# Row maxima of two heads on the two row halves of TensorE, with the attention loop written out

## The reference

```python
q = (x @ Wq.T)  -> (2, 16 heads, 1024, 8);  k, v likewise
attn = softmax((q @ k.T) * 128 ** -0.5, axis=-1)     # 1024 x 1024 for each of 32 heads
attn = attn + rel_bias_table[idx]                    # bias added after the softmax
out  = attn @ v  -> layer norm, * gamma + beta
```

## Time and profile before

| | us |
|---|---|
| median of three runs | 735.07 (731.84 to 736.51) |
| the profiled execution | 732.73 |
| its span | 731.0 |
| PE busy / DVE busy / ACT busy / POOL busy | 676.8 / 533.7 / 381.1 / 104.7 |
| a round of the attention loop | 50.70 |
| the round in which the loop starts its second pass | 56.40 |

### The profile page before, as it was taken

How to read it: one execution, slowest core, us unless ns; L and a number is a source line. 1 busy time by engine, 2 the same in 40 slices (tenths; PEclk the granted TensorE clock), 3 DMA queues, 4 the chain that set the end, 5 groups by cost and what they waited for, 6 DMA issues and landing times.

```text
span 731.0 us, 11045 instructions
## 1 busy us (share of the span) xinstructions
PE 676.8 (93%) x3458; PEld 279.1 (38%) x3458; DVE 533.7 (73%) x956; ACT 381.1 (52%) x687; POOL 104.7 (14%) x100
## 2 busy tenths in 40 slices
PE   7998899999987999999999899999999999988997
PEld 5453545444663522332332232322323322324443
DVE  5579878638799868868868668778688688308744
ACT  3734223324102257767767467667677577882231
POOL 5920211001046220020020020010200202002000
PEclk9999999999999999999999899999999999999999
DMA  8000000000313112012030120030120000000000
GB/s 258 3 0 0 2 0 1 1 0 6 120 66 114 59 48 76 6 55 67 19 98 12 32 96 1 25 100 1 38 87 3 1 0 2 2 1 0 1 29 29
DMA packets 21416, 26.64 MB, mean 36 GB/s; under 512 B 3312, under 2 KB 12016, under 8 KB 21360
## 3 DMA queue, kind: packets, MB, share of 16 engines
q1 hardware_dynamic: 20496, 25.39, 10.8%
q0 software_dynamic: 144, 0.52, 0.2%
q10 hardware_dynamic: 720, 0.00, 0.1%
HBM read 21.52 MB, written 4.19 MB: 35 GB/s over the span
## 4 chain that ended last, share of the span: by engine, by line
PE 70%; DVE 21%; ACT 3%; issue 2%; DVEq 1%; POOL 1%; DMA 1%; POOLq 0%; ACTq 0%
PE banks L1434 17%; PE banks L1357 15%; PE banks L1420 14%; DVE negmax L1034 7%; PE banks L1160 6%; PE banks L1238 4%; PE banks L1281 3%; PE banks L1371 3%; PE banks L1229 2%; DVE arena L892 2%; PE banks L1173 2%; ACT arena L737 1%; DVE arena L942 1%; DVE arena L894 1%; PE banks L1475 1%
## 5 line engine op out<-in xcount | busy, mean ns | idle before, releaser
L1034 DVE TENSOR_REDUCE negmax<-banks 128x1 f32<-128x1024 f32 x256 | 300.5, 1218 | 67.0 <-PE banks L1357 65.8
L737 ACT ACTIVATE arena<-banks 128x512 f32<-128x512 f32 x512 | 271.7, 601 | 143.9 <-PE banks L1420 140.3
L1357 PE MATMUL banks<-arena 72*128 72x512 bf16 x512 | 154.8, 384 | 15.7 <-DVE negmax L1034 15.2
L1420 PE MATMUL banks<-arena 75*128 75x512 bf16 x512 | 159.3, 382 | 6.3 <-ACT arena L737 3.1
L1434 PE MATMUL banks<-arena 128*32 128x512 f32 x1024 | 137.2, 608 | 0.7 <-ACT arena L737 0.7
L1357 PEld LDWEIGHTS banks<-arena 72*128 72x128 bf16 x512 | 36.4, 97 | 146.8 <-DVE negmax L1034 68.1
L1420 PEld LDWEIGHTS banks<-arena 75*128 75x128 bf16 x512 | 48.3, 98 | 93.6 <-ACT arena L737 47.6
L501 POOL TENSOR_TENSOR rstd<-veps,neghalf 128x4 f32<-128x4 f32 (+1 forms) x24 | 27.1, 1129 | 241.4 <-DVE veps L808 189.6
L1238 PE MATMUL banks<-arena,bT 128*128 128x512 f32 x128 | 60.1, 593 | 1.6 <-ACT arena L591 1.6
L591 ACT ACTIVATE arena<-banks 128x512 f32<-128x512 f32 (+1 forms) x56 | 32.1, 595 | 49.3 <-PE banks L1160 19.3
L892 DVE TENSOR_SCALAR arena<-banks,bi 128x512 f32<-128x512 f32 x32 | 23.9, 746 | 33.0 <-PE banks L1238 33.0
(11 more groups left out here) (132 smaller groups left out, 638.2 us busy)
## 6 DMA issues: line engine op xcount, KB each, us to landing
arena<-qk_scratch SPq DMA_DIRECT2D x192, 48.0 KB
arena<-in_tab SPq DMA_DIRECT2D x8, 1024.0 KB, 6.9
qk_scratch<-arena SPq DMA_DIRECT2D x8, 384.0 KB, 2.7
out<-x SPq DMA_DIRECT2D x4, 256.0 KB, 2.3
x<-in_x SPq DMA_DIRECT2D x1, 512.0 KB, 4.5
x<-in_x POOLq DMA_DIRECT2D x1, 512.0 KB, 7.6
arena<-nm_part SPq DMA_DIRECT2D x24, 8.0 KB, 1.9
w_aT<-in_w_aT SPq DMA_DIRECT2D x1, 256.0 KB, 6.5
```

The costliest lines, as they stand in the source:

```text
L737: act.activation(probs[s % 2][:, h, :], score_bank(g, n), ACT.Exp, scale=SCALE).then_inc(exp_done, 1)
L1034: return dve.tensor_reduce(negmax[:, buf, k:k + 1], slot.rearrange("p a b -> p (a b)"), axis=AXX, op=ALU.max, negate=True)
L1357: last = pe.matmul(slot[:, half_, :], qs[0:STACK, buf, h, t * P:(t + 1) * P], ks[0:STACK, buf, h, half_ * HALF:(half_ + 1) * HALF], start= ...
L1420: pe.matmul(score_bank(g, n), ks[0:DEPTH, g % BUFS, h, t * P:(t + 1) * P], qs[0:DEPTH, g % BUFS, h, q * HALF:(q + 1) * HALF], start=True, ...
```

## The change

1. **Maxima by pairs of heads.** Products are cut to the first 64 of 72 partitions for a maximum (the product of the two low parts falls out of it). Beside `qs` and `ks` (partitions 0 to 63, even head of a pair), a new tensor `upper` holds the odd head of the pair in partitions 64 to 127, in memory that is free by then. An item is now 128 rows of two heads against 512 keys: one matmul on partitions 0 to 63 and one on 64 to 127, into the two banks of a slot. There are still 32 such items for a group, with two matmuls each.
2. **Reduction.** DVE's reduction of an item now gives two numbers a row (each over 512) into `negmax_part`; after a group's last item a drain and one more instruction (128 x 32, minimum) join the two halves of the keys.
3. **Loads.** `load_upper` adds 12 transfers a group (six for each pair of heads, of 24 or 16 partitions): on SP between the others, for group 0 on ACT, behind a wait for `qk_stored` and behind ACT's work for the first mixture-of-experts block. The order of heads in the loads is 0, 2, 1, 3.
4. **Step.** Scores of heads 0, 1 and 2, two items, `weigh`, further items, scores of head 3.
5. **Loop.** `Fori` becomes a Python loop on all engines: six rounds written out, all wait targets constants.
6. **Beginning.** `x0[:, 0]` comes in two halves of 256 KB, one by SP, one by ACT; `w_inT` has its own semaphore; a one-column Identity activation runs on ACT as soon as the constants are there.

```diff
+        def load_upper(engine, G, buf, pair):
+            head = bass.ds(G * GW + (2 * pair + 1) * HD, HD)
+            for i in range(NPART):
+                n = NPART if i < NPART - 1 else NPART - 1
+                rows = slice(UPPER + i * NPART * HD, UPPER + i * NPART * HD + n * HD)
+                engine.dma_start(upper[buf][rows, 0, pair, :], scratch[0, i, head, :].unsqueeze(0).broadcast_to([n, HD, S])).then_inc(upper_loaded[buf][pair], 16)
+                engine.dma_start(upper[buf][rows, 1, pair, :], scratch[1, 0:n, head, :]).then_inc(upper_loaded[buf][pair], 16)
...
-            sp.dma_start(x0[:, 0], x_tiles(x_in, 0)).then_inc(x_loaded[0], 16)
+            sp.dma_start(x0[:, 0, 0:TH], x_tiles(x_in, 0)[:, 0:TH]).then_inc(x_loaded[0], 16)
+            sp.dma_start(w_inT[:], w["w_inT"]).then_inc(w_in_loaded, 16)
...
+            act.dma_start(x0[:, 0, TH:NT], x_tiles(x_in, 0)[:, TH:NT]).then_inc(second_half_loaded, 16)
...
             act.wait_ge(consts, N_CONSTS)
+            act.activation(idle[:], tiny[:], ACT.Identity)
...
             ffn(0)
+            act.wait_ge(qk_stored[0], 64)
+            for pair in range(GH // 2):
+                load_upper(act, 0, 0, pair)
             q_and_k(1)
...
-            with act.Fori(0, (GROUPS - 2) // BUFS) as i:
+            for i in range((GROUPS - 2) // BUFS):
...
             def max_item(slot, buf, k):
-                return dve.tensor_reduce(negmax[:, buf, k:k + 1], slot.rearrange("p a b -> p (a b)"), axis=AXX, op=ALU.max, negate=True)
+                pair, t, q = k // (2 * NT), k // 2 % NT, k % 2
+                last = dve.tensor_reduce(negmax_part[:, buf, q, 2 * pair:2 * pair + 2, t], slot, axis=AXX, op=ALU.max, negate=True)
+                if k == MAXES - 1:
+                    dve.drain()
+                    last = dve.tensor_tensor(negmax[:, buf, :], negmax_part[:, buf, 0].rearrange("p h t -> p (h t)"),
+                                             negmax_part[:, buf, 1].rearrange("p h t -> p (h t)"), ALU.min)
+                return last
...
             def max_item(G, g, slot, d, k):
-                for half_ in range(2):
-                    last = pe.matmul(slot[:, half_, :], qs[0:STACK, buf, h, t * P:(t + 1) * P], ks[0:STACK, buf, h, half_ * HALF:(half_ + 1) * HALF],
-                                     start=True, stop=True)
+                if t == 0 and q == 0:
+                    times = (G + d) // BUFS + 1
+                    pe.wait_ge(products_loaded[buf][2 * pair], 16 * 2 * NPART * times)
+                    pe.wait_ge(upper_loaded[buf][pair], 16 * 2 * NPART * times)
+                pe.matmul(slot[:, 0, :], qs[0:UPPER, buf, 2 * pair, t * P:(t + 1) * P], ks[0:UPPER, buf, 2 * pair, q * HALF:(q + 1) * HALF],
+                          start=True, stop=True)
+                return pe.matmul(slot[:, 1, :], upper[buf][UPPER:P, 0, pair, t * P:(t + 1) * P], upper[buf][UPPER:P, 1, pair, q * HALF:(q + 1) * HALF],
+                                 start=True, stop=True)
...
             def step(G, g, s, fill_item, ring):
-                scores(G, g, s, 0)
-                if len(ring) > 0:
-                    fill_item(ring[0])
-                scores(G, g, s, 1)
-                scores(G, g, s, 2)
+                for h in range(GH - 1):
+                    scores(G, g, s, h)
+                for k in ring[:2]:
+                    fill_item(k)
                 if s:
                     weigh(G, g, s - 1)
...
-                if len(ring) > 1:
-                    fill_item(ring[1])
-                scores(G, g, s, 3)
                 for k in ring[2:]:
                     fill_item(k)
+                scores(G, g, s, GH - 1)
```

More of the change, by code:

```diff
@@ L258, in build @@
         tiny = sb("tiny", [P, 1])
+        idle = sb("idle", [P, 1])
         zero_t = sb("zero_t", [P, NT])
@@ L369, in build @@
         products_loaded = [[sem(f"products_loaded{n}{h}") for h in range(GH)] for n in range(BUFS)]
+        upper_loaded = [[sem(f"upper_loaded{n}{p}") for p in range(GH // 2)] for n in range(BUFS)]
         bias_loaded, varying_ready, v_ready = sem("bias_loaded"), sem("varying_ready"), sem("v_ready")
@@ L429, in load_products, with load_head @@
             def load_products(G, buf):
[L431 to L436, removed]
+                load_head(G, buf, 0)
+                if G:
+                    load_upper(sp, G, buf, 0)
+                load_head(G, buf, 2)
+                if G:
+                    load_upper(sp, G, buf, 1)
+                load_head(G, buf, 1)
+                load_head(G, buf, 3)
+            def load_head(G, buf, h):
+                head = bass.ds(G * GW + h * HD, HD)
+                for i in range(NPART):
+                    rows = slice(i * NPART * HD, (i + 1) * NPART * HD)
+                    sp.dma_start(qs[rows, buf, h, :], scratch[0, i, head, :].unsqueeze(0).broadcast_to([NPART, HD, S])).then_inc(products_loaded[buf][h], 16)
+                    sp.dma_start(ks[rows, buf, h, :], scratch[1, :, head, :]).then_inc(products_loaded[buf][h], 16)
             def load_negmax(G, buf):
@@ L572, in round_ @@
                 pool.drain()
-            with pool.Fori(0, (GROUPS - 2) // BUFS) as i:
+            for i in range((GROUPS - 2) // BUFS):
                 for n in range(BUFS):
@@ L1131, in attended @@
                 norm(N_FFN1, b, x)
-            with dve.Fori(0, (GROUPS - 2) // BUFS) as i:
+            for i in range((GROUPS - 2) // BUFS):
                 for n in range(BUFS):
@@ L1513, in _ @@
                 step(0, 0, s, fill_ahead, list(range(start, start + share)))
-            with pe.Fori(0, (GROUPS - 2) // BUFS) as i:
+            for i in range((GROUPS - 2) // BUFS):
                 for n in range(BUFS):
```

19 lines of the change are left out of this document (12 added, 7 removed).

## The result

The changed kernel took 753.58 us (median of 4 runs, 750.97 to 754.53), the kernel before, beside it, 733.93 (4 runs). The ratio is 1.027, with a 95% interval of 1.022 to 1.031: **slower by 2.7%**. The forecast was 739 with a range of 717 to 766; the direction given most chance and the range hold, the size does not: +0.5% was forecast. The profiled execution has a span of 752.7, 21.7 over that of before.

What follows compares the result with a forecast made beforehand. PE was taken as the bound in two-item steps, DVE 0.47 behind. Rounds +7.5, loop -5.7, first maxima +3.5 and beginning -1.0 gave +4.3 on 735.07, so 739 us, range 717 to 766.

Steps and rivals of the forecast that it cites:

- The bound and the chain: Attention step: PE bounds two-item steps, DVE 0.47 behind; head 3's scores to head 2's take 1.06, PE waits 0.40.
- The price of a switch: Attention step: each change into or out of row halves costs 0.11 us, bounds 0 to 0.22.
- The first rival: Attention step: mode changes into row halves cost nothing, a step is 2.72, total 719 us; chance 0.28.
- The overlap of the halves: Maxima: an item's two matmuls on row halves run at once, so it takes 0.22 instead of 0.44.
- The rivals of 0.33 and 0.44 an item: Maxima: halves overlap only in part (756 us, chance 0.25) or not at all (781 us, chance 0.10).
- The sum of a plain step: Attention step with two items: 2.94 us against 2.83, so 0.11 slower a step.
- The one pair with a third item: Attention loop: a three-item step and the next take 6.71 us against 6.72, nothing won.
- A round: Attention rounds: +1.1 us each, +7.5 over seven rounds' worth.
- The loop written out: Edge into the loop's second pass: its cost goes, -5.7 us, bounds 0 to -6; register work gives nothing.
- The first maxima: Stage ahead of the rounds: first item 3.1 to 3.9 later, behind ACT's loads; +3.5 us, bounds 0 to 5.
- The beginning: Kernel start: table load moved and first load halved, first product near 12.1; -1.0 us, bounds -0.3 to -2.
- a rival of 756: Maxima: halves overlap only in part, 0.33 an item, a step 3.16, total 756 us; chance 0.25.

Runs made afterwards that it cites:

- Kernel 2: The kernel before with only the new order of a step, without the row halves: 776.58 us, ratio 1.057.
- Kernel 7: The changed kernel with ACT's copy of the weighted values moved behind head 3's exponential: 749.16 us, ratio 1.021.
- kernel 1: The changed kernel with only the order of a step put back as before, row halves kept: 724.14 us, ratio 0.985 to before.
- kernel 3: The kernel before with only its five hardware loops written out in Python: 727.93 us, ratio 0.991.
- kernels 4 and 5: The changed kernel with group 0's upper loads on SP instead of ACT (751.28 us); with SP waiting until ACT's first six loads have landed (749.22 us, one run).
- kernel 6: The changed kernel with 50 instead of 14 keep-busy products on PE ahead of the first item: 751.13 us (2 runs).
- kernel 8: The kernel before with only the changed beginning (halved load, own semaphore for w_in, idle activation): 732.33 us against 734.34, ratio 0.998.

## Why the prediction was right and where it was not

**The bound and the chain: right.** PE was the bound by 0.47 over DVE, and the chain head 3's scores, exponential, head 2's scores was forecast at 1.06 from start to start; it is 1.08. The forecast wait of 0.40 shows as 0.42: head 2 comes 1.08 behind head 3 where three scores need 0.66. Kernel 2 shows that the order alone makes it.

**The price of a switch: right.** 0.11 was taken over from `weigh`; the rows show 0.10 between whole array and halves. The first rival (no price, 719) falls by its own test: scores of head 2 to the first item is 0.32, not 0.22. The Trainium skill, "TensorEngine Tiling (Array Packing)", Key Properties, states that a change of the tiling mode drains the engine; the trace agrees as far as a price shows at each change, 0.10 by the rows, which the page does not give.

**The overlap of the halves: right, and fully.** 0.22 was forecast for an item; the starts are 0.23 apart, and the two heads' starts within 0.01. The rivals of 0.33 and 0.44 an item fall. "TensorE: Matmul & The Clock Gate", Measured speedup, in the Trainium skill has 3.07 for four row tiles; for two, here, 0.44 becomes 0.23, a loss of the factor 2 no larger than the hundredth to which rows are read.

**The sum of a plain step: right**, 2.94. The one pair with a third item and nothing else in it came to 3.77 + 2.93 = 6.70; 6.71 was forecast.

**A round: the step that failed.** "Together +1.1" was 2.2, and the +7.5 for the rounds and the steps ahead of them was +15.1 (0.8 ahead, 13.4 in the six rounds, 0.9 behind). Two parts were not in the sum. The first is ACT's copy, 0.60 between two exponentials twice a round: +0.36 and +0.30 against the same steps of before, of which 0.1 each is the plain step's. It was hidden while PE led, and the forecast had moved ACT onto the path without asking what else ACT does there. Kernel 7 shows it: 0.45 a round. The second is the step of `turn`. Only two things of `ring` stand ahead of `weigh` now, and there the transposition takes the place of an item, which slips behind `weigh`:

```profile
412.44 0.39 PE L1403 MATMUL banks<-arena 64*128 64x512 bf16 x1
412.44 0.39 PE L1405 MATMUL banks<-arena 64*128 64x512 bf16 x1
412.76 0.28 PE L1410 MATMUL banks<-ident,negmax 128*32 128x128 f32 x1
412.97 1.06 PE L1483 MATMUL banks<-arena 128*32 128x512 f32 x8
414.15 0.39 PE L1403 MATMUL banks<-arena 64*128 64x512 bf16 x1
414.15 0.39 PE L1405 MATMUL banks<-arena 64*128 64x512 bf16 x1
...
416.49 0.39 PE L1403 MATMUL banks<-arena 64*128 64x512 bf16 x1 [0.22 <-DVE negmax_part L1074]
416.49 0.39 PE L1405 MATMUL banks<-arena 64*128 64x512 bf16 x1
416.81 1.06 PE L1483 MATMUL banks<-arena 128*32 128x512 f32 x8
```

Between the two `weigh` three items now need DVE, and the interval is 3.84 where it was 2.98. The forecast counted the items of a step by their number and not by the side of `weigh` on which they fall. That this causes the +0.86 is read from the rows; no run moved `turn` alone. That it comes with the order is shown: kernel 2 has 4.15 there against 3.26 for its plain step, kernel 1 with the halves and the old order 2.93 against 2.72. The steps of `bias` and of what follows it (+0.22, +0.32, then -0.64) also moved, and were not taken apart.

**The loop written out: right**, -5.7, with none of the register work showing; kernel 3 gives -5.6 by its rows. SP's 36 loads a round, priced at nothing, cost nothing: from 285 to 600 no engine waits for a DMA.

**The first maxima: the term that was mis-sized most.** 3.5 was forecast, 9.0 came at the first item and 11.9 at the first scores (less the 0.4 that the kernel was behind at 190). Issue times were right within 0.3. The landing was taken from lone transfers; 48 KB loads that follow one another every 0.72 land in 4.0 to 4.1, and in 7.9 beside a second queue doing the same (kernels 4 and 5). The upper bound of 5, "if the idle PE drops to the lower clock", named a second part and gave it 1.5, and kernel 6 shows 1.6; but the forecast added nothing for it. Most of the rest is the group of 16 products at the lower clock, 1.6, which this execution had and others did not.

**The beginning: right where it was measured, lost later.** The first product came at 12.01 for a forecast of 12.1. The forecast took for granted that the lead lasts. In two profiled executions it was gone by the first round, each time in a stretch where PE, having stood, ran at its lower level: near 73 in the changed kernel, near 234 in kernel 8. In kernel 7, with the same beginning as the changed kernel, the 26 records near 73 took 3.17 and the lead held to 190.

So the terms as they came are: beginning +0.4, first maxima +11.9, rounds +15.1, loop -5.7, together +21.7, against -1.0, +3.5, +7.5 and -5.7. That the range held is luck: it held because it reached to a rival of 756 whose mechanism, a partial overlap, did not happen. The time is near that rival's and its reason is wrong. The direction rests on more: the plain step is longer by the 0.11 forecast, for the reason forecast, though most of the 21.7 comes from what the forecast had too small or left out.

## What to carry to other kernels

When a regrouping takes work out of the shadow of a dependency, the engine at the other end of it is on the path from then on: list everything that this engine does between the two ends, not only the operation that gave the dependency its name. Price a first load by a burst like it, with all queues that are issuing beside it, not by a lone transfer; and keep TensorE at work while it waits, since the wait is paid a second time in its clock. A saving and an order that come in one change should be timed apart: here the halves were worth 2.2 to 4.1 us a round, and the order that came with them cost 4.4 to 6.3.

## What was not expected of the hardware

- **A second queue issuing beside it holds a load up.** A 48 KB load, sixth of a burst with one issue per 0.72, landed in 4.1 us from SP's queue, in 4.0 from ACT's with SP still, in 7.7 to 8.1 from ACT's, in three executions, while SP issued at the same pace. Whether the queues or only the number of loads matter was not tested.
- **The edge of a loop has no fixed price.** Entering the second pass cost 5.7 in the kernel before, 2.7 in kernel 8 and 10.6 in kernel 2, all with the same program up to that edge but for the order of a step in kernel 2 and the beginning in kernel 8. PE stood with "issue" as the cause for 2.95, 2.67 and 4.29; the rest is the lower clock behind it, where eight records of `weigh` took 1.93 and 1.94 instead of 1.06 (kernels before and 2). In kernel 8 the clock stayed up (1.07), and the wait is the whole price. The loop's other edges showed none.
- **The clock makes executions differ.** Behind the same idle time of 3.17 near 73 us, 26 products took 3.17, 4.64 and 5.91 in kernel 7, the changed kernel and kernel 1, which are the same program up to there. A lead of 1 us can't be counted on across such a place.
- **Two row halves overlap without loss**: starts within 0.01, two items 0.23 apart (one product alone is 0.22), 0.10 for each switch to or from the whole array.
